# Expert stages of a language-model tower: blocks taken in pairs, and the 64-feature part of gate and up padded to 128 rows with zeros

## The reference, cut to what matters

```python
# layer 0: one of 8 experts for a token, hidden width 512
oe = silu(xe @ w1[e]) * (xe @ w2[e]) @ w3[e]
# layer 1: the best two of 8 experts, hidden width 384, and a shared expert that every token passes
routed += c[:, None] * (silu(x @ Wg.T) * (x @ Wu.T) @ Wd.T)
out = routed + silu(x @ sg.T) * (x @ su.T) @ sd.T
```

## Time and profile before

| what | us |
|---|---|
| runs of the kernel before: median (lowest to highest of 3) | 2190.5 (2176.0 to 2199.99) |
| profiled execution: span from the first to the last instruction | 2094.5 |
| median less span: what lies around the instructions | 96.0 |
| TensorE busy in the span | 1846.6 (88%) |
| VectorE busy | 1119.3 (53%) |
| ScalarE busy | 639.8 (31%) |
| GpSimd busy | 299.5 (14%) |

### The profile page before, as it was taken

One profiled execution on the slowest core, in us unless ns is written; L12 is line 12 of the kernel. 1 busy time (PEld: TensorE's weight loads), 2 busy tenths in 40 slices (PEclk: granted clock), 3 DMA queues, 4 the chain that ended last, 5 costly groups with the idle time before them and its releaser, 6 DMA issues. The chain is left out here.

```text
span 2094.5 us, 29605 instructions
## 1 busy us (share of the span) xinstructions
PE 1846.6 (88%) x8344; PEld 933.7 (45%) x8345; DVE 1119.3 (53%) x2583; ACT 639.8 (31%) x1068; POOL 299.5 (14%) x311
## 2 busy tenths in 40 slices
PE   5779998999999976099999699997949999999996
PEld 3412332332333255045554367667815555555553
DVE  5878997987999346012222355544642233333356
ACT  3404665665766831011111111110111111111111
POOL 6530000000000011500000310001127100000056
PEclk9857999999999986579999699998759999999998
DMA  3466222231330050101110100004023111111134
GB/s 88 143 107 211 32 31 31 34 47 19 44 41 1 1 184 0 62 23 32 33 32 28 49 16 8 8 0 156 1 87 100 47 41 40 41 40 41 41 96 118
DMA packets 95611, 112.75 MB, mean 54 GB/s; under 512 B 12590, under 2 KB 81842, under 8 KB 94898
## 3 DMA queue, kind: packets, MB, share of 16 engines
q1 hardware_dynamic: 63102, 74.28, 14.4%
q0 software_dynamic: 10752, 22.03, 3.5%
q10 hardware_dynamic: 21696, 15.74, 3.0%
HBM read 64.72 MB, written 47.28 MB: 53 GB/s over the span
## 5 line engine op out<-in xcount | busy, mean ns | idle before, releaser
L509 DVE TENSOR_REDUCE sa_half_max<-psum 128x1 f32<-128x512 f32 x768 | 494.6, 687 | 63.5 <-PE psum L613 43.9
L567 ACT ACTIVATE sa_probs<-psum 128x1024 f32<-128x1024 f32 x384 | 372.3, 1022 | 167.4 <-PE psum L604 165.8
L613 PE MATMUL psum<-k_stack,q_stack 96*128 96x512 bf16 x768 | 285.5, 410 | 26.1 <-PEq L397 15.2
L1308 PE MATMUL psum<-w_e_up_b,ex_xt_b 64*128 x576 | 286.4, 578 | 0.0
L1306 PE MATMUL psum<-w_e_up_a,ex_xt_a 128*128 x576 | 259.3, 532 | 4.9 <-ACT ex_xt_b L1180 2.6
L1185 ACT ACTIVATE ex_silu<-psum 128x384 f32<-128x384 f32 (+1 forms) x144 | 74.8, 520 | 590.6 <-PE psum L1308 590.6
L604 PE MATMUL psum<-q_stack,k_stack 97*128 97x512 bf16 x768 | 231.2, 385 | 6.3 <-ACT sa_probs L567 5.4
L1219 DVE TENSOR_TENSOR ex_g<-ex_silu,psum 128x384 f32<-128x384 f32 (+1 forms) x144 | 85.2, 592 | 248.1 <-PE psum L1308 244.3
L1225 DVE COPY ex_g_t<-psum 128x384 f32<-128x384 f32 (+1 forms) x144 | 85.6, 595 | 235.8 <-PE psum L1325 235.4
L636 PE MATMUL psum<-sa_probs,sa_v_ext 128*32 128x512 f32 x1536 | 206.6, 610 | 0.6 <-ACT sa_probs L567 0.6
L613 PEld LDWEIGHTS psum<-k_stack,q_stack 96*128 96x128 bf16 x768 | 75.0, 98 | 281.1 <-issue 147.8
(11 more groups left out here) (207 smaller groups left out, 1903.3 us busy)
## 6 DMA issues: line engine op xcount, KB each, us to landing
ex_x<-x_rows ACTq DMA_DIRECT2D x144, 96.0 KB
y_rows<-ex_y SPq DMA_DIRECT2D x112, 96.0 KB, 1.6
q_stack<-qk_parts SPq DMA_DIRECT2D x66, 128.0 KB, 4.2
k_stack<-qk_parts SPq DMA_DIRECT2D x66, 128.0 KB, 7.1
x_rows<-sa_zeros SPq DMA_DIRECT2D x1, 6912.0 KB, 35.2
qk_parts<-ep_parts SPq DMA_DIRECT2D x16, 384.0 KB, 3.2
w_e_up_a<-e_up_a SPq DMA_DIRECT2D x1, 4096.0 KB, 12.6
x_rows<-sa_zeros SPq DMA_DIRECT2D x1, 3840.0 KB, 13.7
```

The source lines that it names most:

```text
L509: nc.vector.tensor_reduce(half_max[:, g, hd, qt, half:half + 1], slot, AX.X, ALU.max).then_inc(ring_free[r], 1)
L567: nc.scalar.activation(probs[:, st % 2, 2 * pair:2 * pair + 2, :], ps[:, 2 * pair:2 * pair + 2, :], ACT.Exp, scale=SCALE0).then_inc(exp_do ...
L613: last = nc.tensor.matmul(ps[:, 4 + r, :], qst[0:SK, g, hd, qt * P:(qt + 1) * P], kst[0:SK, g, hd, half * 512:(half + 1) * 512], start=Tru ...
L1308: nc.tensor.matmul(dst, xt_b[:, u, :], up_b[:, which, bass.ds(e, 1), :].rearrange("p o f -> p (o f)"), start=False, stop=True).then_inc(do ...
```

## The change

- Blocks are taken in pairs. Loads, stores, the copy of y, the copy of x and the transposes of x are done for a pair at once. `x` has 256 columns for a block, the last 64 of them cleared once. The load moves from ScalarE's queue to SyncE's, where it is written out for every pair.
- The transposed x has 128 rows for both pieces (`xt`), and `up_b` has 128 rows: its 64 rows stand there twice, since the weights are loaded a second time into rows 64 to 127. They meet zeros, so gate and up are the same sums. All weight loads of the stage now have 128 rows and 128 columns.
- The order on TensorE for pair k is: look up both experts of the pair; the four 64-feature matmuls (`half_rows`); look up both experts of the pair before; its down projection; the four 128-feature matmuls (`full_rows`); transposes of x of the pair after; transposes of g of this pair. One pair is one pass of the loop.
- Shared blocks name their expert by a constant and have no lookup.
- In layer 1's tail, VectorE's steps are written out with a table of how many `mix` follow each.

```diff
+MIXED_IN_TAIL = (1, 1, 2, 2, 2, 2, 1)
...
-        up_a, up_b, down = (dst for dst, _ in s.expert_weights)
-        x = sb("x", [P, 2, D])
-        xt_a = sb("xt_a", [P, 2, P])
-        xt_b = sb("xt_b", [DB, 2, P])
+        up_a, up_b, down = s.up_a, s.up_b, s.down
+        x = sb("x", [P, 2, 2 * P])
+        xt = sb("xt", [P, 2, 2 * P])
...
-        PS_X, PS_GATE, PS_UP, PS_G, PS_Y = 0, 1, 3, 5, 6
+        PS_X, PS_GATE, PS_UP, PS_G, PS_Y = 0, 1, 3, 5, 7
+        def over(eng, lo, hi, body):
+            if hi - lo == 1:
+                body(lo)
+            elif hi > lo:
+                with eng.Fori(lo, hi) as k:
+                    body(k)
...
+            def load(k):
+                if k == FIRST:
+                    sp.wait_ge(rows_placed, START + 1)
+                first = 2 * k + (blocks_of(k_top) if k < FIRST else -BEFORE if k < LAST else 0)
+                sp.wait_ge(x_ps, START + k)
+                pair = x_rows[first * P:(first + 2) * P, :].rearrange("(u p) d -> p u d", p=P)
+                sp.dma_start(x[:, :, 0:D], pair).then_inc(loaded, 16)
+            def store(k):
+                first = 2 * k - BEFORE
+                sp.wait_ge(y_done, START + k + 1)
+                sp.dma_start(y_rows[first * P:(first + 2) * P, :].rearrange("(u p) d -> p u d", p=P), y[:]
+                             ).then_inc(stored, 16)
+            load(0)
+            load(1)
+            for k in range(PAIRS + 1):
+                if FIRST <= k - 1 < LAST:
+                    store(k - 1)
+                if k + 2 < PAIRS:
+                    load(k + 2)
+            sp.wait_ge(stored, START + 16 * (LAST - FIRST))
...
+            def copy_x(k):
+                act.wait_ge(x_ps, START + k + 1)
+                act.wait_ge(up_ps, START + 2 * k)
+                nc.scalar.copy(xt[:].rearrange("p u c -> p (u c)"), ps[:, PS_X, :]).then_inc(xt_done, 1)
+            def activate(k, u):
+                act.wait_ge(gate_ps, START + 2 * k + u + 1)
+                act.wait_ge(g_done, START + 2 * k)
+                nc.scalar.activation(silu[:, u, :], ps[:, PS_GATE + u, 0:F], ACT.Silu).then_inc(silu_done, 1)
+            def step(k):
+                activate(k, 0)
+                activate(k, 1)
+                copy_x(k + 1)
+            copy_x(0)
+            over(act, 0, PAIRS - 1, step)
+            activate(PAIRS - 1, 0)
+            activate(PAIRS - 1, 1)
...
+            def step_after(finish):
+                def step(k):
+                    finish(k - 1)
+                    product(k, 0)
+                    product(k, 1)
+                    copy_g(k, 0)
+                    copy_g(k, 1)
...
+            nc.vector.memset(x[:, :, D:2 * P], 0.0).then_inc(cleared, 1)
+            product(0, 1)
+            copy_g(0, 0)
+            copy_g(0, 1)
+                over(dve, 1, PAIRS, step_after(copy_y))
+                copy_y(PAIRS - 1)
+                lead, tail = add_shared(0), add_shared(LEAD - (BEFORE + blocks_of(k_top)))
+                over(dve, 1, FIRST + 1, step_after(lead))
+                over(dve, FIRST + 1, LAST + 1, step_after(copy_y))
+                mixed = 0
+                for k in range(LAST + 1, PAIRS):
+                    step_after(tail)(k)
+                    for n in range(mixed, mixed + MIXED_IN_TAIL[k - LAST - 1]):
+                        mix(n)
+                    mixed += MIXED_IN_TAIL[k - LAST - 1]
+                tail(PAIRS - 1)
+                for n in range(mixed, ROUNDS * BUFS):
+                    mix(n)
...
+            class Shared:
+                def __init__(self, k):
+                    pass
+                def half(self, u, which):
+                    return up_b[:, which, NE - 1, :]
+                def up(self, u, which):
+                    return up_a[:, which, NE - 1, :]
+                def down(self, u, c):
+                    return down[:, NE - 1, c, :]
+            class Routed:
+                def __init__(self, k):
+                    self.e = [pe.value_load(s.owner[0:1, bass.ds(2 * k + u, 1)], min_val=0, max_val=E - 1)
+                              for u in range(2)]
+                def half(self, u, which):
+                    return up_b[:, which, bass.ds(self.e[u], 1), :].rearrange("p o f -> p (o f)")
+                def up(self, u, which):
+                    return up_a[:, which, bass.ds(self.e[u], 1), :].rearrange("p o f -> p (o f)")
+                def down(self, u, c):
+                    return down[:, bass.ds(self.e[u], 1), c, :].rearrange("p o d -> p (o d)")
+            def transpose_x(k):
+                pe.wait_ge(loaded, START + 16 * (k + 1))
+                pe.wait_ge(xt_done, START + k)
+                for u in range(2):
+                    nc.tensor.transpose(ps[:, PS_X, 2 * u * P:(2 * u + 1) * P], x[:, u, 0:P], s.ident[:])
+                    last = nc.tensor.transpose(ps[:, PS_X, (2 * u + 1) * P:(2 * u + 2) * P], x[:, u, P:2 * P], s.ident[:])
+                last.then_inc(x_ps, 1)
+            def half_rows(k, w, first=False):
+                pe.wait_ge(xt_done, START + k + 1)
+                if not first:
+                    pe.wait_ge(g_done, START + 2 * k)
+                for u in range(2):
+                    for which, bank in ((0, PS_GATE), (1, PS_UP)):
+                        nc.tensor.matmul(ps[:, bank + u, 0:F], xt[:, u, P:2 * P], w.half(u, which),
+                                         start=True, stop=False)
+            def full_rows(k, w):
+                for u in range(2):
+                    for which, bank, done in ((0, PS_GATE, gate_ps), (1, PS_UP, up_ps)):
+                        nc.tensor.matmul(ps[:, bank + u, 0:F], xt[:, u, 0:P], w.up(u, which), start=False, stop=True
+                                         ).then_inc(done, 1)
+            def transpose_g(k):
+                for u in range(2):
+                    pe.wait_ge(g_done, START + 2 * k + u + 1)
+                    for c in range(FC):
+                        last = nc.tensor.transpose(ps[:, PS_G + u, c * P:(c + 1) * P], g[:, u, c * P:(c + 1) * P],
+                                                   s.ident[:])
+                    last.then_inc(g_ps, 1)
+            def down_project(k, w):
+                pe.wait_ge(y_done, START + k)
+                for u in range(2):
+                    pe.wait_ge(g_t_done, START + 2 * k + u + 1)
+                    for c in range(FC):
+                        last = nc.tensor.matmul(ps[:, PS_Y, u * D:(u + 1) * D], g_t[:, u, c * P:(c + 1) * P],
+                                                w.down(u, c), start=(c == 0), stop=(c == FC - 1))
+                last.then_inc(y_ps, 1)
+            def step(kind, before=None, more=True):
+                def body(k):
+                    w = kind(k)
+                    half_rows(k, w)
+                    down_project(k - 1, (before or kind)(k - 1))
+                    full_rows(k, w)
+                    if more:
+                        transpose_x(k + 1)
+                    transpose_g(k)
+                return body
+            kind = Shared if layer else Routed
+            pe.wait_ge(cleared, START + 1)
+            transpose_x(0)
+            w = kind(0)
+            half_rows(0, w, first=True)
+            full_rows(0, w)
+            transpose_x(1)
+            transpose_g(0)
+            if layer == 0:
+                over(pe, 1, PAIRS - 1, step(Routed))
+            else:
+                over(pe, 1, FIRST, step(Shared))
+                step(Routed, Shared)(FIRST)
+                over(pe, FIRST + 1, LAST, step(Routed))
+                step(Shared, Routed)(LAST)
+                over(pe, LAST + 1, PAIRS - 1, step(Shared))
+            step(kind, more=False)(PAIRS - 1)
+            down_project(PAIRS - 1, kind(PAIRS - 1))
...
-    names = [f"e{layer}_{n}" for n in ("up_a", "up_b", "down")]
+    up_a, up_b, down = (a[f"e{layer}_{n}"] for n in ("up_a", "up_b", "down"))
     with ExitStack() as ctx:
         new_sem = ctx.enter_context(semaphores(nc))
-        pairs = [(ctx.enter_context(nc.sbuf_tensor("w_" + n, a[n].shape, F32))[:], a[n]) for n in names]
-        yield pairs, new_sem(f"experts{layer}_loaded")
+        def sb(name, shape):
+            return ctx.enter_context(nc.sbuf_tensor(f"w_e{layer}_{name}", shape, F32))
+        tiles = sb("up_a", up_a.shape), sb("up_b", [P] + list(up_b.shape[1:])), sb("down", down.shape)
+        loads = [(tiles[0][:], up_a), (tiles[1][0:DB], up_b), (tiles[1][DB:P], up_b), (tiles[2][:], down)]
+        yield tiles, loads, new_sem(f"experts{layer}_loaded")
```

More of the change, by code:

```diff
@@ L1128, in _ @@
             if layer == 1:
-                for u in range(2):
-                    pool.wait_ge(two["stored"][u], START + 16 * (LAST - FIRST))
+                pool.wait_ge(stored, START + 16 * (LAST - FIRST))
                 for c in range(ROUNDS):
@@ L1146, in _ @@
         def _(sp):
-            def store(u, k):
-                sp.wait_ge(two["y"][u], START + k + 1)
```

(30 more changed lines are left out.)

164 lines of the change are left out of this document (29 added, 135 removed).

## The result

The changed kernel takes 2218.5 us (median of 4 runs, 2207.7 to 2225.6) beside 2185.2 us for the kernel before (4 runs, 2176.0 to 2200.0): a ratio of 1.014, 95% interval 1.009 to 1.019. It is slower by 1.4%, clear of the noise; the forecast was 2232, 1.9% slower. A second set gave 2218.3 beside 2190.7, ratio 1.015 (1.009 to 1.021).

A forecast was written before the change was run, and what follows sets the result against it. TensorE bounds the routed blocks, GpSimd the ends of lead and tail. Layer 0 +15.5 and layer 1 +26 give +41.5: span 2094.5 to 2136, plus 96.0 is 2232 us, 1.9% slower; range 2150 to 2264.

The forecast's parts named there:

- The padding: TensorE, routed blocks: 128-row weights remove four changes between 128-row and 64-row weights, 0.79 us a block, 1.57 a pair.
- Lookups behind a late wait: End of each pair: two lookups run only after the g-transpose wait; half_rows starts at 5.8 instead of 3.9 us.
- L610 behind L604: Layer 0 trace: L610's register instruction starts only when the held L604 matmul starts, so lookups cannot run during a wait.
- the second product: Pair's second block, from full_rows' start: up ends 2.56, product done 3.37, second g transposes start 3.51 instead of 3.32 us.
- Rival 3: Routed part: idling lowers the clock; a third of the time at 1.2 GHz adds 150, giving 2380 us; chance 0.04.
- its mark at 0.95: Routed part: a granted clock below 0.95 would refute the forecast.
- Layer 0: Layer 0's routed blocks: 19 pair-to-pair steps at 0.69 us are +13, ends add some 2.5; +15.5 us.
- the 13 of the steps: Layer 0: 19 steps from pair to pair, each 0.69 us longer (12.9 against 12.25), +13 us.
- +2.5 for the ends: Layer 0: larger first load and x copy, and the last pair's two lookups ahead of down, add some 2.5 us.
- Layer 1, routed part: Layer 1's routed pairs: 35 steps at 0.73 us are +25.6; with small terms at start and end, +26 us.
- Lead and tail: Layer 1's shared pairs at about 8.8 us stay beside GpSimd's scatters and 82 us of gathers; no change.
- The 96.0 around the span: Outside the profiled span: 96.0 us, added unchanged to spans 2094.5 and 2136 to give 2190.5 and 2232.

The follow-up runs named there:

- the version of 8.8 us pairs: Changed kernel with silu table and lookups ahead, layer 1's lead held until scatters landed (late-results test): 2102.4 us beside 2096.3, ratio 1.002; again 2101.7 beside 2097.2.

## Why the prediction was right, and where not

**The padding** (0.79 a block): right; 0.74 measured by itself.

**Lookups behind a late wait** (half_rows 1.9 late; pair 10.4 and 12.9): right in mechanism, and a little too large. Without the table load the pairs take 10.30 and 12.79. TensorE is idle for 1.67 us and not 1.9; with the lookups moved 0.20 of that is left, and 1.47 to 1.48 a pair is gone. The start of the next reads at 1715.2, behind the wait and not beside it, is what L610 behind L604 had said. By the Trainium skill's Perfetto Trace Analysis, Tensor Engine Instruction (MATMUL, LD_WEIGHTS), the sequencer would have gone on; the trace of after shows it held until 1714.7.

**Missing: the table load.** The step that failed is that of the second product ("done at 3.37", g transposes at 3.51). They come at 3.42 for the first and 3.89 for the second block's in the changed kernel, with ScalarE loading its table from 0.91 to 2.20. With the load ahead of the loop the second block's come at 3.45, so the rest of that step was right. Before, one silu stood ahead of ScalarE's loop and took the load; in the changed code only a copy stands there, so the load went into the loop body, 70 times. The diff showed that and I read it for times and not for what the compiler would place there. It cost 0.43 a pair. A term of the same kind is told by the Trainium skill, ScalarE: Activation LUTs, What ACT_TABLE_LOAD costs, with 1283 ns; for the load itself the trace agrees (1283 ns, and silu starts 0.01 us behind it).

**Missing: the clock.** Rival 3 was put at a third of the routed time; what came was some 8% of it: nine times 3.4 us at the 1.2 GHz level, 15 us, a mean of 0.96 where the forecast had set its mark at 0.95. With 1.67 us idle in 10.73 and another 0.24 ahead of the g transposes it falls every third or fourth pair; with 1.67 in 10.30 and no 0.24 it fell once; with 0.20 in 9.26 never.

**Layer 0** (+15.5): too large; +3.7 measured, +0.9 to the first profile's 302.2. Its pairs do cost 12.83 - 12.26 = 0.57 each, 11.4 in all, near the 13 of the steps. But the fill is cheaper: before, gate and up of the first block and gate of the second run at half clock (2.0 us from one pair of records to the next, from 900.0 to 913.4), after it is half_rows alone (5.08). From the first x transpose to the last down it is 255.2 before (in the profile with late results), 10 above 40 x 6.13, and 258.4 after, 2 above 20 x 12.83. I had put +2.5 for the ends; it is -8.

**Layer 1, routed part** (+26): +45.7. 36 x 1.05 = 38 and the half-clock steps 15 make 53, and the 36 pairs from their first half_rows on do take 401.2 us for 348.5. What is left over from the lead behind the last scatter gives 7.6 back (65.2 for 72.8). The forecast lacks 0.43 x 36 = 15 for the table and 15 for the clock. Its terms were also added up wrongly: 25.6 - 0.9 - 2 + 2.2 + 2 + 0.5 + 0.3 is 27.7 and not 26, which would have made the forecast 2234.

**Lead and tail** ("GpSimd-bound, nothing"): right without late results (the version of 8.8 us pairs ends 93.7 us behind its first gather, have 91.8), wrong with them. There the lead leaves 65 to 73 us behind the last scatter, and the tail took 118.0 before and 112.1 after, its gathers 104.5 and 102.6 for the 82 that the forecast kept. Shared pairs take 9.08 and not 8.8, by the same table load.

**The 96.0 around the span**: wrong as a reading. It was time inside of other executions. It did little harm because both kernels have the late results at nearly the same cost, which the forecast did not know: the change rewrites the lead and the tail as well. That is luck.

So the total is in part luck. Counted in spans, 30 us that were not foreseen (table and clock in the routed part) stand against -36 that were not either (layer 0 -12, the rest of the routed part -10, the tail -6, the stages ahead and between -8, which are not the change's): 41.5 + 30 - 36 = 36, the spans' difference (the medians differ by 33).

## What to carry to other kernels

What TensorE's sequencer has to do between its last wait and the next matmul is paid as far as no queued matmul covers it: here 2.2 us of it left a gap of 1.6, and with the two lookups ahead of the wait, in registers, the gap was 0.2. A lookup that already lay beside matmuls was worth nothing. A change that bundles two ideas is to be priced as two: here the padding was worth 4%, and the pairs as they were written gave back, by difference, some 5.5. When a loop is written anew, look at which activation stands ahead of it, since that decides whether its table load is paid once or in every turn. And when a profile's span is far below the timed runs, compare it with a second profile of the same kernel, stage by stage, before you carry the difference over as time around the span: here 1.7 us lay around it, not 96.

## What the runs showed of the hardware that I had not expected

TensorE's results reached ScalarE and VectorE tens of us late while GpSimd's indirect DMAs ran: 34 us for the down result and 65 for the x transposes in the lead of the changed kernel, one after another at 4 to 12 us, in order. The kernel before had it in three sets of runs and not in two, with the same code, and it cost 90 us of 2190: 61 in the lead and 26 in the tail. Within a set all of its runs agree (2174 to 2210 us in the three, 2084 to 2110 in the two), so it goes with the set, and so perhaps with the chip. That the DMAs cause it is not shown: the version meant to test that ran twice, both times in a set without it. Whether TensorE itself was slow or only the signal of its being done isn't shown either. And in a loop with a gap of 1.6 us in every turn, and 0.24 more ahead of the g transposes, the granted clock fell now and again (mean 0.96, TensorE busy for 248.7 of 300 us); without the 0.24 it fell once (0.99, 252.1 of 300), and with the gap at 0.20 it stood at 1.00 (285.3 of 300).
